# Idle transposes, early selectors and a value product beside the copies in the prologue of a four-layer kernel

## The chip, the cores and the metric

One core of a Trainium2 chip runs one program. The metric is the device time of one execution in microseconds, as the median of the runs. The engines are TensorE (PE; its weight loads are shown as PEld), VectorE (DVE), ScalarE (ACT), GpSimd (POOL) and the sync engine (SP), which issues most transfers.

## The reference, cut to what matters

Four sequences of 512 tokens of width 256 go through four layers: a causal attention block (L0), a small expert adapter (L1), a routed feed-forward block (L2), and an attention block with bias, mask and a scale and shift made from a time step (L3). The change lies in the start of L0 for sequence 0 and in the sine embedding of L3.

```python
def _L0_cond_ref(x, gate_score, Wq, bq, Wk, bk, Wv, bv, ...):
    h = layernorm(x, gamma1, beta1)
    Q, K, V = h @ Wq + bq, h @ Wk + bk, h @ Wv + bv      # 16 heads of 16
    scores = Q K^T / 4, causal
    ctx = softmax(scores) @ V
    ...
def _L3_cond_ref(src, src_mask, timestep, attention_bias, W_ada, ...):
    emb = silu(_sin_emb(timestep)) @ W_ada + b_ada       # scale and shift of L3
    x = _ln(src) * (1.0 + scale) + shift
    ...
```

## The kernel before, in words

The work is laid out by ticks. A tick from 0 on is a unit: one head of one block of 128 query tokens; an attention has 64 units, and there are eight attentions (four sequences, two layers with attention). In each unit every engine takes its standing work (scores and transposes on TensorE, the maximum on VectorE in `maxima`, the exponential on ScalarE, copies of the transposed probabilities on one of the last two), and then the dense steps that the plan put on that tick with `at(tick, engine, step, ...)`. Every engine runs its own list strictly in order; semaphores join them. Ticks below 0 are the prologue, which has dense steps alone. `copy_sides` decides from the planned loads which engine copies in which unit.

The prologue of before, for sequence 0:
- `plan_norm(-20, ...)` on VectorE: statistics (L998), a chain of small instructions for the inverse root, and `apply` (L1039), which writes h in four pieces.
- `turn_tokens` (L1236): eight transposes of h into dense banks 0 and 1, then `feature_half` on VectorE and ScalarE, which writes hT.
- `qk` 0 and 1 (L1258): the Q and K products of the first eight heads, 4 matmuls each, then `v` 0 (L1272), the value product of the first two blocks of tokens, 8 matmuls. The other Q and K products, `qk` 2 and 3, come at ticks 2 and 3.
- The Q and K rows are split into three bf16 parts: `hi` (ScalarE, L860), `rest` (VectorE, L1076), `mid` (ScalarE, L865), `lo` (VectorE, L1082).
- `restack` (L1367): 48 small matmuls with selection matrices put the parts of the first 256 tokens into eight banks. ScalarE copies four banks to `qs` (L893) and signals early_q_done, VectorE copies four to `ks` (L968) and signals early_k_done. `selectors` (L958 to L962) makes the selection matrices from the identity: a memset, a reduction, 16 small copies.
- `v` 1 (L1272): the value product of the other two blocks. It needs dense bank 0, which holds one of the four K banks of the restack, and waits for all four K copies. `values_out` (L1092) copies it out.
- `setup_sin` on ScalarE (L899, L901) takes a sine and an exponential of a small table that GpSimd has made; each needs a table load. Its result is read by `setup_silu` at tick 20.
- GpSimd makes the identity first (L649, L650), then clears `va` (L657, L658), and then works on the angles (L671 to L698).

scores(0) waits for all eight copies of the restack. The norm of sequence 1 starts at tick -1 and its `qkv0` at tick 6. Banks: `score_bank` is bank 0 and 1, `turn_bank` 2 and 3, `ctx_bank` 4, `dense_bank` 5 to 7.

Of the kernel before, what the change touches and what calls it, by code (L numbers as in the profile page):

```python
# [27 lines left out]
P = 128  # L28
# [63 lines left out]
def at(tick, engine, step, *args):  # L92
    EVENTS.append((tick, engine, step, args))


def plan_norm(t, s, k):


    for i in range(2):
        at(t + i, "v", "stats", s, k, i)  # L100
    for i in range(RSQRT_STEPS):
        at(t + 2 + i // SLOTS, f"v{i % SLOTS}", "rsqrt", s, k, i)
    for i in range(2):
        if k in (3, 4, 5):
            at(t + 3 + i, "v", "apply", s, k, i)
            at(t + 5 + i, "v", "apply_late", s, k, i)
        else:
            at(t + 5, "v", "apply", s, k, i)
    if k == 1:
        at(t + 6, "p", "res_l0", s)  # L110
    if k == 6:
        at(t + 6, "p", "res_l3", s)


def plan_turn(t, s, k):
    at(t, "pe", "turn_tokens", s, k)
    at(t + 1, "v", "feature_half", s, k)
    at(t + 1, "a", "feature_half", s, k)


def plan_qkv(t, s, l, second=6, late=4):

    for c in range(2):
        for i in (2 * c, 2 * c + 1):
            u = t + second * c
            at(u + i % 2, "pe", "qk", s, l, i)
            at(u + 1, "a", "hi", s, l, i)
            at(u + 2, "v", "rest", s, l, i)
            at(u + 3, "a", "mid", s, l, i)
            at(u + 4, "v", "lo", s, l, i)  # L130
            at(u + 4, "sp", "parts", s, l, i)
    at(t + 2, "pe", "v", s, l, 0)
    at(t + 3, "v", "v", s, l, 0)
    at(t + late, "pe", "v", s, l, 1)
    at(t + late + 1, "v", "v", s, l, 1)


def plan_ffn(t, s, f):
# [14 lines left out]
        at(t + i + 1, "v", "residual", s, l, i)  # L153


def qkv0(t, s, second=6, late=4):

    plan_turn(t, s, 0)
    plan_qkv(t + 3, s, 0, second, late)


def block0(t, s):
# [23 lines left out]
def qkv3(t, s):  # L186

    plan_turn(t, s, 4)
    plan_qkv(t + 3, s, 1)
# [9 lines left out]
def norm(k):  # L199
    return lambda t, s: plan_norm(t, s, k)  # L200
# [3 lines left out]

STACKS_AT = [(-2, 11)] + [(-28, 4)] * 2 + [(-20, 4)] + [(-28, 4)] * 3 + [(-20, 4)]
BESIDE = [
    [(-1, norm(0), 1), (6, qkv0, 1), (24, norm(0), 2)],
    [(11, qkv0, 2), (12, norm(1), 0), (23, block0, 0), (48, norm(3), 0), (55, block2, 0)],
    [(8, norm(4), 0), (15, norm(5), 0), (22, norm(1), 1), (23, qkv3, 0), (35, block0, 1), (42, norm(0), 3), (60, norm(3), 1)],
    [(3, block2, 1), (20, norm(4), 1), (23, qkv0, 3), (27, norm(1), 2), (34, norm(5), 1), (36, block0, 2), (61, norm(3), 2)],  # L210
    [(11, qkv3, 1), (12, norm(6), 0), (23, block2, 2), (40, block3, 0), (41, norm(4), 2), (48, norm(5), 2)],
    [(11, qkv3, 2), (12, norm(1), 3), (23, block0, 3), (48, norm(3), 3), (55, block2, 3)],
# [7 lines left out]
        at(UNITS * _a + _t, "sp", "stack", _s, _l, _c)  # L220
plan_norm(-20, 0, 0)
at(-14, "v", "setup_scale")
qkv0(-14, 0, 13, 8)
at(-12, "v", "selectors")
at(-12, "a", "setup_sin")
for _e in ("pe", "v", "a"):
    at(-6, _e, "restack")
at(20, "v", "setup_silu")
# [111 lines left out]
def build(nc, T, out):  # L340
    with ExitStack() as ctx:
        def sb(name, shape, dt=F32):
            return ctx.enter_context(nc.sbuf_tensor(name, shape, dt))

        def sem(name):
            return ctx.enter_context(nc.semaphore(name))


        ident = sb("ident", [P, P])
# [79 lines left out]
        score_bank, turn_bank, ctx_bank, dense_bank = bank[0:2], bank[2:4], bank[4], bank[5:8]  # L429
# [11 lines left out]
        early_k_done = sem("early_k_done")  # L441
# [56 lines left out]
        def unit(U):  # L498

            a, u = divmod(U, UNITS)  # L500
            l = ATTENTIONS[a][1]
            c, t, e, j = u // (2 * NT * GH), u // (2 * GH) % NT, u // GH % 2, u % GH
            return a, l, c, t, e, j, HH * c + 2 * j + e, (t + 1) * P if l == 0 else S
# [5 lines left out]
        def prob_of(U):  # L509

            _, l, _, _, _, _, _, n = unit(U)
            return prob[:, U % 3, 0:n] if l == 0 else bias[:, bias_pair(U) % BIAS_RING, U % 2, :]

        early_q_bank = [score_bank[0], score_bank[1], turn_bank[0], turn_bank[1]]
        early_k_bank = [ctx_bank, dense_bank[2], dense_bank[0], dense_bank[1]]

        def res_count(s, layer):

            name, n = {0: ("res_l0", 2), 2: ("res_l2", 1), 3: ("res_l3", 1)}[layer]
            total = 0  # L520
            for _, _, step, args in sorted((t, i, st, a) for i, (t, e, st, a) in enumerate(EVENTS)
                                           if e == "p" and st.startswith("res")):
                total += NT * (2 if step == "res_l0" else 1)
                if step == name and args[0] == s:
                    return total
# [685 lines left out]
        def _(pe):  # L1211
# [51 lines left out]
            def v_rows(s, l, i):  # L1263
                if ATT[s, l] == 0:
                    pe.wait_ge(load_v, 16 * LOADS_V)
                    if i:
                        pe.wait_ge(early_k_done, 4)
                if i:
                    pe.wait_ge(rest_done, 4 * ATT[s, l] + 2)
                for t in (2 * i, 2 * i + 1):  # L1270
                    for c in range(ND):
                        mm = pe.matmul(dense_bank[V_BANK[i]][:, (t % 2) * D:(t % 2 + 1) * D], hT[:, c, t * P:(t + 1) * P],  # L1272
                                       wv[l][:, c, :], start=c == 0, stop=c == ND - 1)
                mm.then_inc(v_psum, 1)
# [82 lines left out]
            def restack():  # L1357
# [4 lines left out]
                for side, banks, signal in ((0, early_q_bank, early_q), (1, early_k_bank, early_k)):  # L1362
                    for e in range(2):
                        for x in range(3):
                            for g in range(4):
# [3 lines left out]
                                if x == 2 and e == 1:  # L1369
                                    mm.then_inc(signal, 1)  # L1370

            def scores(U):
                a, l, c, t, e, j, hd, n = unit(U)
                if U == 0:
                    pe.wait_ge(early_q_done, 4)
                    pe.wait_ge(early_k_done, 4)
                if U == 2 * HH or U % (UNITS // 2) == 0 and U:
                    pe.wait_ge(stack_in[hd // HH], 96 * (a + 1))
                if U >= 2:
                    pe.wait_ge(p_done if unit(U - 2)[1] == 0 else max_done, U - 1)  # L1380
                mm = pe.matmul(score_bank[U % 2][:, 0:n], qs[:, hd, t * P:(t + 1) * P], ks[:, hd, 0:n],  # L1381
                               start=True, stop=l == 1)
                if l == 0:
                    mm = pe.matmul(score_bank[U % 2][:, n - P:n], identb[:], causal[:], start=False, stop=True)  # L1384
                mm.then_inc(s_psum, 1)
# [32 lines left out]
            def spread_sums(p):  # L1418
# [4 lines left out]
                for w in range(2):  # L1423
# [2 lines left out]

            steps = dense_steps("pe")
            do = {"turn_tokens": turn_tokens, "qk": qk, "v": v_rows, "project": project, "hidden": hidden,
                  "ff_out": ff_out, "turn_expert": turn_expert, "down": down, "expert": expert, "up": up, "setup": setup, "restack": restack}
            pe.wait_ge(consts, 2)  # L1430
            for U in range(FIRST, max(LAST + 1, ALL_UNITS + NORM_AT + 1)):
                if U == 0:
# [59 lines left out]
```

## Time and profile before

| | |
|---|---|
| median of 3 runs | 1169.03 us (1167.12 to 1172.2) |
| the profiled execution | 1163.56 us, span of its instructions 1161.5 us |
| mean granted TensorE clock | 0.959 of full speed |
| PE busy | 997.7 us, 86% of the span |
| VectorE busy | 730.8 us, 63% |
| ScalarE busy | 694.2 us, 60% |
| GpSimd busy | 454.1 us, 39% |

Times of the trace count from the first instruction. A busy PE is not a PE at its peak. The granted clock is in parts of full speed, 0.5 is 1.2 GHz and 1.0 is 2.4 GHz; until about 15 us the record shows 1.00, while the matmuls' durations are those of the low level.

### The profile page before, as it was taken

What the parts mean: (1) busy time and instruction counts of PE and PEld (TensorE: products, weight loads), DVE (VectorE), ACT (ScalarE), POOL (GpSimd) and SP (SyncE); (2) the same over time, 40 slices, a digit from 0 to 9 for tenths busy, and PEclk for the clock granted to TensorE, in tenths of its full rate; (3) what the DMA queues carried; (4) which work ended last, traced back from release to release, by engine and by line L of the source; (5) the groups of instructions that cost most, each with busy time, mean ns of one, the idle gap of its engine ahead of it and who ended that gap; (6) DMA issues with size and microseconds to landing.
All of it is one profiled execution on the core that took longest, in us unless ns stands there. A gap on an engine that the chain in (4) does not pass through costs nothing.

```text
span 1161.5 us, 22288 instructions
## 1 busy us (share of the span) xinstructions
PE 997.7 (86%) x7668; PEld 658.7 (57%) x7668; DVE 730.8 (63%) x1964; ACT 694.2 (60%) x1608; POOL 454.1 (39%) x694
## 2 busy tenths in 40 slices
PE   4878889897889898798889998897996899799768
PEld 3435557465556575466546565575573557557545
DVE  5677773737755738846773668638649864764750
ACT  3566564664675755676565755656754775675731
POOL 8300020000530374561072006847737564894920
PEclk8899999998999998899999999899897899999989
DMA  6868425133261634854626128575393387944600
GB/s 175 224 157 187 74 73 113 34 84 62 63 140 46 146 122 127 198 177 149 130 75 148 37 90 209 183 166 194 104 226 104 121 225 224 219 141 150 214 1 19
DMA packets 118354, 154.79 MB, mean 133 GB/s; under 512 B 12956, under 2 KB 80924, under 8 KB 118244
## 3 DMA queue, kind: packets, MB, share of 16 engines
q1 hardware_dynamic: 113636, 147.04, 47.3%
q0 software_dynamic: 1936, 3.97, 1.4%
q10 hardware_dynamic: 2672, 2.36, 0.6%
q8 instruction: 63, 1.03, 0.4%
q14 instruction: 47, 0.39, 0.1%
HBM read 134.47 MB, written 18.88 MB: 132 GB/s over the span
## 4 chain that ended last, share of the span: by engine, by line
PE 51%; DVE 18%; ACT 15%; issue 9%; DMA 4%; POOL 4%; DVEq 0%; ACTq 0%; POOLq 0%
PE bank L1307 14%; PE bank L1296 9%; PE bank L1399 7%; PE bank L1258 5%; PE bank L1413 5%; PE bank L1381 4%; POOL bias L798 4%; DMA bias<-in_fside_Bx16xSxS 3%; DVE mrow L1142 3%; ACT gT L874 3%; DVE bias L1148 3%; ACT bias L827 2%; ACT prob L824 2%; ACT L874 2%; ACT L827 2%
## 5 line engine op out<-in xcount | busy, mean ns | idle before, releaser
L798 POOL TENSOR_TENSOR bias<-bias,negmask 128x256 f32<-128x256 f32 x512 | 335.9, 687 | 259.2 <-DMA bias<-in_fside_Bx16xSxS 252.6
L827 ACT ACTIVATE bias<-bias,mrow 128x512 f32<-128x512 f32 x256 | 184.1, 719 | 209.3 <-DVE mrow L1148 207.8
L1148 DVE CUSTOM_DVE_ANT_0 bias<-bank,bias 128x512 f32<-128x512 f32 x256 | 175.4, 687 | 186.5 <-PE bank L1381 175.3
L824 ACT ACTIVATE prob<-bank,mrow 128x128 f32<-128x128 f32 (+3 forms) x256 | 134.7, 527 | 193.1 <-DVE mrow L1142 191.6
L1142 DVE TENSOR_REDUCE mrow<-bank 128x1 f32<-128x128 f32 (+3 forms) x256 | 124.5, 488 | 164.5 <-PE bank L1384 163.1
L1381 PE MATMUL bank<-ks,qs 128*128 128x512 bf16 (+3 forms) x512 | 180.3, 352 | 49.2 <-ACT prob L824 34.5
L1399 PE MATMUL bank<-ident,bias 128*128 128x128 f32 x1024 | 164.7, 286 | 54.0 <-ACT pT L835 43.8
L1399 PEld LDWEIGHTS bank<-ident,bias 128*128 128x128 f32 x1024 | 125.2, 146 | 123.9 <-ACT bias L827 71.3
L1296 PE MATMUL bank<-hT,w 128*128 128x512 f32 x384 | 182.6, 606 | 2.0 <-ACT hT L851 0.9
L1307 PE MATMUL bank<-w,gT 128*128 128x256 f32 x768 | 174.3, 381 | 0.0
L1307 PEld LDWEIGHTS bank<-w,gT 128*128 128x128 f32 x768 | 142.5, 190 | 20.2 <-issue 2.7
L1156 DVE COPY pT<-bank 128x512 f32<-128x512 f32 (+3 forms) x237 | 136.5, 576 | 6.4 <-PE bank L1399 5.9
L835 ACT ACTIVATE pT<-bank 128x512 f32<-128x512 f32 (+3 forms) x275 | 139.9, 509 | 1.1 <-PE bank L1399 1.1
L1399 PE MATMUL bank<-ident,prob 128*128 128x128 f32 x640 | 117.9, 283 | 14.2 <-ACT pT L835 8.8
L1413 PE MATMUL bank<-pT,va 128*32 128x128 f32 x3328 | 124.1, 287 | 4.4 <-DVE ctxn L1175 3.3
L1381 PEld LDWEIGHTS bank<-ks,qs 128*128 128x128 bf16 x512 | 50.5, 99 | 127.0 <-ACT prob L824 62.9
L1413 PEld LDWEIGHTS bank<-pT,va 128*32 128x32 f32 x3328 | 87.7, 114 | 28.1 <-issue 25.6
L1296 PEld LDWEIGHTS bank<-hT,w 128*128 128x128 f32 x384 | 68.3, 194 | 61.4 <-issue 59.7
L1399 PEld LDWEIGHTS bank<-ident,prob 128*128 128x128 f32 x640 | 70.9, 144 | 38.5 <-issue 28.9
L757 POOL TENSOR_TENSOR x<-x,xy 128x256 f32<-128x256 f32 x16 | 13.0, 842 | 154.1 <-DVE h L1039 154.1
L768 POOL TENSOR_TENSOR xy<-xy,l2row 128x256 f32<-128x256 f32 x16 | 12.1, 786 | 145.5 <-PE bank L1236 145.5
L874 ACT ACTIVATE gT<-bank,b 128x512 f32<-128x512 f32 x96 | 59.9, 685 | 10.2 <-PE bank L1296 9.8
(155 smaller groups left out, 1140.6 us busy)
## 6 DMA issues: line engine op xcount, KB each, us to landing
bias<-in_fside_Bx16xSxS SPq DMA_DIRECT2D x128, 512.0 KB, 4.6
w<-in_L_cond_W SPq DMA_DIRECT2D x16, 1024.0 KB, 5.6
qs<-q_parts SPq DMA_DIRECT2D x30, 384.0 KB, 10.3
ks<-k_parts SPq DMA_DIRECT2D x30, 384.0 KB, 11.7
q_parts<-parts SPq DMA_DIRECT2D x80, 128.0 KB
k_parts<-parts SPq DMA_DIRECT2D x48, 128.0 KB
w<-in_L_cond_Wi SPq DMA_DIRECT2D x4, 1024.0 KB, 5.0
w<-in_L_cond_Wo SPq DMA_DIRECT2D x4, 1024.0 KB, 5.6
```

The lines of the kernel that those rows point to most:

```text
L798: pool.tensor_tensor(b_n, b_n, negmask[:, t, keys], ALU.add).then_inc(masked, 1)
L824: act.activation(prob_of(U), score_bank[U % 2][:, 0:n], ACT.Exp, bias=mrow[:, U % ROW_RING:U % ROW_RING + 1], accum_out=rsum[:, U % ROW_RI ...
L827: act.activation(prob_of(U), prob_of(U), ACT.Exp, scale=-1.0, bias=mrow[:, U % ROW_RING:U % ROW_RING + 1], accum_out=rsum[:, U % ROW_RING: ...
L835: act.activation(pT[:, U % PT_RING, 0:n // P, :], turn_bank[U % 2][:, 0:n].rearrange("p (k q) -> p k q", q=P), ACT.Identity).then_inc(pt_a, 1)
L1142: v.tensor_reduce(m, score_bank[U % 2][:, 0:n], AX_X, ALU.max, negate=True).then_inc(max_done, 1)
L1148: v.tensor_tensor_reduce(out=prob_of(U), in0=score_bank[U % 2][:], in1=prob_of(U), scale=-1.0, scalar=3e38, op0=ALU.add, op1=ALU.min, accu ...
L1156: v.tensor_copy(pT[:, U % PT_RING, 0:n // P, :], turn_bank[U % 2][:, 0:n].rearrange("p (k q) -> p k q", q=P)).then_inc(pt_v, 1)
L1296: mm = pe.matmul(dense_bank[FF_BANK[j]][:], w1[:, c, j * P:(j + 1) * P], hT[:, c, :], start=c == 0, stop=c == ND - 1)
L1307: mm = pe.matmul(dense_bank[FF_OUT_BANK[t // 2]][:, (t % 2) * D:(t % 2 + 1) * D], gT[:, j, t * P:(t + 1) * P], w2[:, j, :], start=j == 0, ...
L1381: mm = pe.matmul(score_bank[U % 2][:, 0:n], qs[:, hd, t * P:(t + 1) * P], ks[:, hd, 0:n], start=True, stop=l == 1)
L1399: mm = pe.transpose(turn_bank[U % 2][:, k * P:(k + 1) * P], prob_of(U)[:, k * P:(k + 1) * P], ident[:])
L1413: mm = pe.matmul(ctx_bank[32 * j:32 * (j + 1), t % 2 * P:(t % 2 + 1) * P], v_h, pT[:, (GH * w + j) % PT_RING, k, :], start=e == 0 and k == ...
```

## The change

`selectors` moves from tick -12 to tick -21, ahead of the norm of sequence 0. `setup_sin` moves from tick -12 to -5, behind the restack's copies on ScalarE. TensorE gets a new step, `idle_turns`, which transposes the identity into the first score bank; nothing reads the result. It stands at tick -15 with 28 transposes and at tick -8 with 10. The banks of the early K copies change places, so that dense bank 0 is copied first, and `v` 1 waits for one K copy and not for four. The copy-out of `v` 1 for sequence 0 moves from tick -2 to tick 2 (the new argument `copy`). The norm of sequence 1 moves from tick -1 to 2, and its `qkv0` from 6 to 8. With the plan's loads the side of the copies changes in 11 of the first 20 units.

```diff
-def plan_qkv(t, s, l, second=6, late=4):
+def plan_qkv(t, s, l, second=6, late=4, copy=1):
...
     at(t + late, "pe", "v", s, l, 1)
-    at(t + late + 1, "v", "v", s, l, 1)
+    at(t + late + copy, "v", "v", s, l, 1)
...
-def qkv0(t, s, second=6, late=4):
+def qkv0(t, s, *places):
...
-    plan_qkv(t + 3, s, 0, second, late)
+    plan_qkv(t + 3, s, 0, *places)
...
-    [(-1, norm(0), 1), (6, qkv0, 1), (24, norm(0), 2)],
+    [(2, norm(0), 1), (8, qkv0, 1), (24, norm(0), 2)],
...
-qkv0(-14, 0, 13, 8)
-at(-12, "v", "selectors")
-at(-12, "a", "setup_sin")
+qkv0(-14, 0, 13, 8, 5)
+at(-15, "pe", "idle_turns", 28)
+at(-8, "pe", "idle_turns", 10)
+at(-21, "v", "selectors")
+at(-5, "a", "setup_sin")
...
-        early_k_bank = [ctx_bank, dense_bank[2], dense_bank[0], dense_bank[1]]
+        early_k_bank = [dense_bank[0], ctx_bank, dense_bank[2], dense_bank[1]]
...
                     if i:
-                        pe.wait_ge(early_k_done, 4)
+                        pe.wait_ge(early_k_done, 1)
...
+            def idle_turns(n):
+
+                for _ in range(n):
+                    pe.transpose(early_q_bank[0][:, 0:P], ident[:], ident[:])
```

## Rows read from the trace of the kernel before

**Rows 1.** The page: the chain that ended last, by engine.

```profile
PE 51%; DVE 18%; ACT 15%; issue 9%; DMA 4%; POOL 4%; DVEq 0%; ACTq 0%; POOLq 0%
```

**Rows 2.** The chain in order of time, first 80 us: start us, length us, what.

```profile
4.41 1.42 DVE stats L998 x4
...
9.21 1.96 PE bank L1236 x8
...
12.18 5.18 PE bank L1258 x8
17.35 1.74 PE bank L1272 x8
19.21 0.76 DVE va L1092 x2
19.97 1.21 DVE parts L1082 x2
21.23 2.02 PE bank L1367 x48
...
25.95 3.42 PE bank L1272 x8
29.49 0.76 DVE va L1092 x2
30.24 0.66 DVE stats L998 x2
...
31.13 0.47 ACT prob L824 x2
```

**Rows 3.** Timeline, VectorE and ScalarE: start us, us, engine line op out<-in xcount.

```profile
12.18 0.70 DVE L958 MEMSET bias<- 128x768 uint32 x1
13.33 1.58 DVE L962 CAST bias<-bias 128x32 bf16<-128x32 f32 x16
14.86 1.28 ACT L901 ACT_TABLE_LOAD   x1
16.16 0.21 ACT L901 ACTIVATE bias<-bias 128x8 f32<-128x8 f32 x1
22.19 2.06 ACT L893 ACTIVATE qs<-bank 128x512 bf16<-128x512 f32 x4 [2.67 <-PE bank L1367]
23.36 2.48 DVE L968 CAST ks<-bank 128x512 bf16<-128x512 f32 x4 [2.19 <-PE bank L1367]
```

**Rows 4.** Timeline, GpSimd and VectorE at the start.

```profile
1.54 1.38 POOL L657 MEMSET va<- 128x1536 f32 x1
9.88 0.64 POOL L682 TENSOR_SCALAR bias<-bias 128x4 f32<-128x4 f32 x1
9.94 0.43 DVE L951 TENSOR_SCALAR wq<-wq 128x512 f32<-128x512 f32 x1
```

**Rows 5.** Line L1236 to 14 us (duration ns min/median/max, first and last start); four K products.

```profile
L1236 PE MATMUL bank<-ident,h x8: 421/421/447, 9.2 to 10.7; 128*128 128x128 f32 x8
...
47.58 1.88 PE L1258 MATMUL bank<-hT,wk 128*128 128x512 f32 x4
```

**Rows 6.** Windows: length, PE, PEld, DVE, ACT, POOL busy (x), PEclk, DMA share, GB/s.

```profile
18.60:22.00 3.40, 1.25 (x31) 0.82 (x33) 2.22 (x5) 0.63 (x1) 3.40 (x6) 1.00 0.67 193
22.00:25.40 3.40, 1.25 (x28) 0.60 (x16) 2.04 (x4) 2.06 (x4) 3.40 (x7) 0.51 0.72 159
990.00:1004.00 14.00, 11.37 (x134) 7.89 (x135) 11.71 (x31) 10.86 (x27) 13.03 (x20) 1.00 0.80 210
```

**Rows 7.** The last of these windows, transposes of the probabilities (L1399) alone.

```profile
990.00:1004.00 14.00, 7.32 (x48) 4.99 (x46) 1.00 0.80 210
```

**Rows 8.** Timeline: qk 2 at unit 2, and the first maximum over 256 keys (unit 8).

```profile
31.88 3.22 PE L1258 MATMUL bank<-hT,wq 128*128 128x512 f32 x4
...
43.81 0.41 DVE L1142 TENSOR_REDUCE mrow<-bank 128x1 f32<-128x256 f32 x1
```

**Rows 9.** Window of units 0 to 7, from the first exponential to unit 8's maximum.

```profile
31.10:43.80 12.70, 9.83 (x45) 4.80 (x45) 9.13 (x35) 6.55 (x25) 6.71 (x10) 0.82 1.01 220
```

More of the change, by code:

```diff
@@ L1428, in _ @@
             do = {"turn_tokens": turn_tokens, "qk": qk, "v": v_rows, "project": project, "hidden": hidden,
-                  "ff_out": ff_out, "turn_expert": turn_expert, "down": down, "expert": expert, "up": up, "setup": setup, "restack": restack}
+                  "ff_out": ff_out, "turn_expert": turn_expert, "down": down, "expert": expert, "up": up, "setup": setup, "restack": restack, "idle_turns": idle_turns}
             pe.wait_ge(consts, 2)
```

## The prediction

> **What bounds the kernel now.** I read the page's chain first: half of it is TensorE, a fifth VectorE, 9% issue [rows 1]. After the first tokens no single engine sets the pace; that stretch is bounded by hand-overs, and the diff leaves it alone but for the planner's first 30 ticks. So a gain can only be a start of attention 0 that comes earlier and is then carried through. Next I read the chain of the first 80 us in order of time [rows 2]. The reader should see four pieces ahead of the first exponential at 31.13: the norm of sequence 0 (4.41 to 9.21), twelve us of products and their splitting into parts (to 21.23), the restack products with the four K copies behind them (to 25.95), then a value product of 3.42 us with its copy (0.76) and half of the next sequence's statistics (0.66) on VectorE, before which the first maximum can't run. The last two pieces are 9.9 us long and most of what they hold is an order, not a dependency. All of it is judged against the profiled execution, 1163.56 us (span 1161.5); the median of the three runs is 1169.03, 5.5 higher, and I take the saving off that.
>
> **Selectors first.** The same 18 instructions move from 12.18 to the front of VectorE's queue, where they wait for the identity alone. They take 2.73 us: from the memset at 12.18 to the end of the sixteenth copy, 13.33 + 1.58 = 14.91 [rows 3]. The identity is there at 1.5 (GpSimd's next instruction starts at 1.54 [rows 4]), so they end at about 4.3, and the statistics start at 4.41 on a transfer: cost 0. They were not on the chain where they stood (14.91 is long before 21.23), so removing them gains 0 too. The cover is thin, 0.1 us. Beside them GpSimd now runs two memsets of 1.38 us, from 1.54 on [rows 4]. The trace doesn't show that pairing. It does show that the two engines can hold each other up: a GpSimd instruction on 128x4 took 0.64 us at 9.88, as VectorE scaled 128x512 in SBUF at 9.94 [rows 4]. Bounds: 0, and one memset's length, 1.4 us, ahead of the statistics. I take 0, because in their old place the copies kept an even pace of 0.1 us each beside GpSimd's small instructions [rows 3]; 1.4 is a rival. On this the Trainium skill (SBUF — State Buffer, section Summary: rules for kernel authors) says that a VectorE instruction in a two-port mode and a GpSimd one block each other completely, the later one waiting for the end of the first; by it the copies would wait for the second memset and the sum would be 1.4 us worse. The trace agrees on the small GpSimd instruction, and shows nothing of the reverse.
>
> **28 turns of the identity.** Eight transposes of this size began between 9.2 and 10.7, 0.214 us apart, at the low clock [rows 5]. So 28 take 6.0 us, from 1.5 to 7.5, before the tokens come at 9.21: they delay nothing unless each takes over 0.27 us (a lone one is recorded with 0.42 [rows 5]). Do they make the first products fast? Four Q products with four K products took 5.18 us in the chain while four at the full clock take 1.88 [rows 2, 5], so the first four ran at 1.2 GHz; at 2.4 they would give 1.7 us, and the token turns 0.7 (1.96 us for what then follows the tokens within 0.3 us each). Upper bound 2.4 us. But between 7.5 and 9.2 TensorE idles, or longer if the clock rises on the way and the turns end sooner, then works in small pieces on the tokens and idles again until hT is there, 12.18 [rows 2]. What idling does is in the trace: after v(0) ended at 19.1 the engine stood until 21.23, and the granted clock, 1.00 until 22.0, was 0.51 after it [rows 6]. I take 0 of the 2.4 us: the clock rises under the turns and is gone before the products. Then the start at 12.18, the high clock from about 15, v(0), the splitting, and the restack at 21.23 all stay.
>
> **setup_sin behind the copies.** ScalarE's two table loads (1.28 us each) and two small activations (0.21 each) [rows 3] leave 12 to 16.4. The first hi may start sooner for it, but the chain goes from both products (to 17.35) through v(0) to VectorE [rows 2], past ScalarE's wait, so 0. In their new place they follow the Q copies, which end at 22.19 + 2.06 = 24.25 [rows 3]: 2.98 us, to 27.25. Its output is wanted at tick 20 only. Queued behind it is the first exponential.
>
> **10 turns.** They fill 19.1 to 20.2 of the gap before the restack (10 x 0.107 at the high clock), delaying nothing. The idle time there falls from 2.1 to 1.0 us, and I expect the clock to stay high: the restack products (2.02, the second half at the low clock [rows 2, 6]) give back 0.4 us (0 to 0.6), and v(1) takes 1.74 as v(0) did, not 3.42 [rows 2].
> Whether turns hold the clock at all is a question of its own. From 990 to 1004 it stood at 1.00 while 7.3 of 11.4 busy us were transposes [rows 6, 7]: they at least don't break it. The Trainium skill (TensorE: Matmul & The Clock Gate, section Part 4: PE-mode transpose) says that the full clock doesn't engage for transposes, which don't count as a busy engine the same way. By that rule neither set of turns does anything; this is a rival below. The trace doesn't decide it, since matmuls stand between those transposes.
>
> **v(1) beside the K copies.** It now waits for one K copy, not four, since the bank that it needs is copied first. The four take 2.48 us [rows 3]. With the restack 0.4 earlier they run from 22.95 to 25.45; v(1) starts at 23.65 and ends at 25.4, hidden. scores(0) comes at 25.5, where v(1) alone ended at 25.95 + 3.42 = 29.37 before: 3.8 less.
>
> **The VectorE queue ahead of the first maximum.** The values' copy (tick -2 to 2) and the norm of sequence 1 (tick -1 to 2) go behind it. So the maximum runs at 25.8 to 26.1, where it ended at about 31.1: 5.0 earlier. Here setup_sin becomes the later one: the exponential starts at 27.25 and not at 31.13. Saved at this point: 3.9 us, and 1.15 us of the maximum's lead is lost to the table loads.
>
> **What it costs later.** 0.76 us of copy and the norm of a sequence (for sequence 0 it took 4.8 us from first statistics to tokens [rows 2]) now lie in units 2 to 7, three ticks later, qkv0(1) two ticks later. Before, most of the norm lay under four products of 3.22 us at the low clock [rows 8], which held the scores back; after them it lies where VectorE has the splitting to do as well. Bounds: -1.0 (the clock stays high under those products and more than pays for it) and 2.5 (half the norm comes into the open). I take 0.6: from 31.1 to 43.8, units 0 to 7, VectorE was busy for 9.1 of 12.7 us [rows 9], so most of it finds room. SP's queue: the parts of (1,0) are issued two ticks later, wanted in attention 1 only.
> Sum: 3.9 - 0.6 = 3.3 saved. 1163.56 - 3.3 = 1160.3 beside the profiled run, 1169.0 - 3.3 = **1165.7** as a median.
>
> **The rivals.**
> *The clock lasts into the first products*: 2.4 us more, all else the same; saved 5.7, 1163.3. For it: only small gaps stand between 9.2 and 12.2. Against it: the fall at 22.0.
> *GpSimd's memset holds the selectors*: 3.3 - 1.4 = 1.9 saved, 1167.1. Against it: no VectorE instruction of this trace's beginning is stretched.
> *Turns don't count*: the restack stays as it is, v(1) runs from 24.1 for 3.42 to 27.5, the first exponential at 28.1: 3.0 - 0.6 = 2.4 saved, 1166.6. The small difference is because setup_sin would have eaten that time anyway.
> *The displaced norm is exposed* (the slower side): values' copy and norm, 0.76 + 4.8 = 5.6 us, lie on VectorE between unit 2 and the tokens of sequence 1, whose products every later unit waits behind. If all of it is in the open, 3.9 - 5.6 = 1.7 lost, 1170.7. It decides from the point at which over 3.9 of the 5.6 us are uncovered. Against it: in the 12.7 us before unit 8's maximum (43.81 [rows 8]) VectorE had 3.6 us free [rows 9], with most of the norm already in its work.
>
> **How the numbers follow.** Forecast 0.43 (its own range 1163 to 1168.5), clock lasts 0.22, turns don't count 0.11, memset 0.12, norm exposed 0.12. 0.5% is 5.8 us, about what a measurement of this kernel can tell from no change. Faster by more needs under 1163.2: half of the second case, the edge of the first and the -1.0 bound together, 0.21. Slower by more needs over 1174.9: only an exposed norm with a fallen clock, 0.04. Within: 0.75. The three runs shown differ by 5 us, so the range reaches past the cases: 1161 to 1170.5.
>
> **What would show it.** Right: statistics still at 4.4, the first Q product of 12.2 at half speed, restack at 21.2, scores(0) near 25.5, the first exponential directly behind the second table load near 27.3, unit 8's maximum 3 to 4 us before 43.8. Wrong: statistics at 5.8 (memset), a Q product that starts at 11.5 and takes 0.43 (clock lasts), v(1) of over 3 us (turns don't count), unit 8 no earlier than 43 (norm exposed). A saving of over 6 us at unit 8 would mean that I put too low what the clock gives back.

## The result, and the profile after

| | before | changed |
|---|---|---|
| median of 5 runs | 1167.19 us (1167.0 to 1172.2) | 1160.35 us (1157.17 to 1162.13) |
| ratio | | 0.9925 [0.99, 0.9951] |
| the profiled execution | 1163.56, span 1161.5 | 1160.35, span 1158.5 |

The changed kernel is 6.8 us faster where 3.3 were forecast: 0.6 us under the range's low end of 1161, and on the side to which I gave 0.21. The forecast median was 1165.7, 5.3 us above the measured one. Of these, 1.8 are the starting point (1169.03 from three runs, 1167.19 from five) and 3.5 are the saving itself. Beside the profiled run of before the difference is only 3.2 us, which looks like the forecast. It isn't, as the experiments show.

The page of the changed kernel, its span and its busy times:

```profile
span 1158.5 us, 22278 instructions
...
PE 988.7 (85%) x7619; PEld 664.2 (57%) x7706; DVE 730.7 (63%) x1961; ACT 695.4 (60%) x1611; POOL 452.6 (39%) x694
...
PE 44%; DVE 21%; ACT 15%; issue 9%; POOL 5%; DMA 4%; another core or an unknown queue 1%; SPq 0%; DVEq 0%; ACTq 0%; POOLq 0%
```

The 9 us less that TensorE is busy (988.7 against 997.7) are no saving: this trace has 7619 matmuls for 7706 weight loads, so 87 matmul records are missing, and none are in the trace of before (7668 of each). A second trace of before lacks 87 too and has 986.7. TensorE's share of the chain falls from 51% [rows 1] to 44%, but second traces of both kernels have 46%. The page tells little; the chain and the single units tell more.

The chain of the changed kernel in order of time, first 63 us (start, length, what); lines have moved by 2 against before:

```profile
2.85 2.45 DVE bias L964 x16
5.30 1.32 DVE stats L1000 x4
...
9.92 1.98 PE bank L1238 x8
...
12.91 6.59 PE bank L1260 x8
19.50 1.74 PE bank L1274 x8
...
23.38 0.94 PE bank L1369 x24
24.34 2.06 ACT qs L895 x4
26.42 1.28 ACT L901
27.94 1.28 ACT L903
29.45 0.36 ACT prob L826 x2
30.25 1.72 PE bank L1260 x4
...
62.80 1.88 PE bank L1349 x4
```

Three things differ from [rows 2]. The selectors' sixteen copies now stand in the chain ahead of the statistics, which start at 5.30, not at 4.41. The restack begins 2.15 us later than before (23.38 against 21.23). From there to the first exponential it takes 6.0 us (23.38 to 29.35) where before took 9.9, and v(1) and its copy are gone from it; the two table loads (L901, L903) are the last thing before the exponential.

Timeline of the same stretch, VectorE, GpSimd and TensorE (start, length, engine, line, operation, out<-in):

```profile
2.85 2.45 DVE L964 CAST bias<-bias 128x32 bf16<-128x32 f32 x16
2.94 1.53 DVE L964 CAST bias<-bias 128x32 bf16<-128x32 f32 x5
...
2.97 1.38 POOL L660 MEMSET va<- 128x1536 f32 x1
...
1.53 5.01 PE L1377 MATMUL bank<-ident 128*128 128x128 f32 x28 [1.53 <-POOL ident L652]
...
12.91 3.75 PE L1260 MATMUL bank<-hT,wq 128*128 128x512 f32 x4 [1.03 <-ACT hT L853]
...
23.38 1.49 PE L1369 MATMUL bank<-parts,bias 32*128 32x256 bf16 x48 [1.06 <-DVE parts L1084]
25.79 1.97 PE L1274 MATMUL bank<-wv,hT 128*128 128x256 f32 x8 [0.92 <-issue]
```

The second line is the same view in the window 3.3 to 4.36 us, and holds the five of the sixteen copies that are under way there. The reader should see the copies lasting 2.45 us beside a GpSimd memset, where they took 1.58 without one [rows 3], with five of them begun by 3.28 and done only at 4.38 to 4.47, right behind the memset's end at 4.35; 28 transposes in 5.0 us and the first Q product after them still at half speed (3.75 for four matmuls that take 1.88 at the full clock [rows 5]); and v(1) at 1.97, beside the K copies.

Where the time went shows best in the start of the exponential of a unit, in us. "Second trace" is the trace of the whole kernel run once more (`f_before2` and `f_after2` below, on two different chips); the last column is the normalisation (the write of ctxn) of the last attention:

| trace | unit 0 | unit 10 | unit 18 | unit 22 | unit 39 | last ctxn |
|---|---|---|---|---|---|---|
| before | 31.13 | 48.02 | 63.50 | 72.54 | 95.42 | 1114.55 |
| before, second trace | 30.76 | 47.65 | 63.14 | 72.19 | 95.09 | 1117.72 |
| changed | 29.35 | 43.65 | 57.66 | 66.13 | 87.95 | 1111.87 |
| changed, second trace | 27.87 | 42.34 | 58.23 | 66.71 | 88.65 | 1110.70 |

The changed kernel leads by 1.8 us at unit 0 (forecast: 3.9), 4.4 at unit 10, 5.8 at unit 18 and 7.5 at unit 39. So most of the gain arises after the prologue, in units 0 to 22, in the term for which I had put down a loss of 0.6. By stretches, this pair gains 2.3 us from unit 0 to 5, 0.3 to unit 10, 1.5 to unit 18, 0.6 to unit 22 and 1.1 to unit 39. From there the lead stays between 5.7 and 7.5 until 904 us, and then falls to 2.7 at 1114.55. That last fall is the luck of one execution of before: its second trace agrees with the first within 0.8 us up to 740 us, and is 3.2 us later at the last normalisation. Against it the leads of the changed kernel's two traces there are 5.9 and 7.0:

```profile
1114.55 0.42 DVE L1175 TENSOR_TENSOR ctxn<-bank,spread 128x256 f32<-128x256 f32 x1 [3.06 <-ACT spread L843]
```

```profile
1117.72 0.42 DVE L1175 TENSOR_TENSOR ctxn<-bank,spread 128x256 f32<-128x256 f32 x1 [3.11 <-ACT spread L843]
```

These are the last normalisations in the timelines of before and of its second trace.

### The profile page after: what moved, and what is told of

The parts are those of the page before. It is cut to its first block, busy times and chain, and to the rows that moved or that the text cites. A ratio compares the mean times of both kernels' runs of the same rounds, so it can differ in the third digit from the quotient of the medians.

```text
span 1158.5 us, 22278 instructions
## 1 busy us (share of the span) xinstructions
PE 988.7 (85%) x7619; PEld 664.2 (57%) x7706; DVE 730.7 (63%) x1961; ACT 695.4 (60%) x1611; POOL 452.6 (39%) x694
## 3 DMA queue, kind: packets, MB, share of 16 engines
q8 instruction: 63, 1.03, 0.4%
## 4 chain that ended last, share of the span: by engine, by line
PE 44%; DVE 21%; ACT 15%; issue 9%; POOL 5%; DMA 4%; another core or an unknown queue 1%; SPq 0%; DVEq 0%; ACTq 0%; POOLq 0%
PE bank L1309 14%; PE bank L1298 8%; PE bank L1406 6%; POOL bias L800 4%; PE bank L1260 4%; DMA bias<-in_fside_Bx16xSxS 4%; PE bank L1420 3%; DVE bias L1150 3%; DVE mrow L1144 3%; ACT gT L876 3%; PE bank L1388 3%; ACT bias L829 2%; DVE stats L1000 2%; ACT prob L826 2%; ACT L876 2%
## 5 line engine op out<-in xcount | busy, mean ns | idle before, releaser
L1388 PE MATMUL bank<-ks,qs 128*128 128x512 bf16 (+3 forms) x425 | 146.4, 345 | 45.6 <-ACT prob L826 32.5
```

## The experiments

The question became: which part makes the 7 to 8 us, and why in units 0 to 22? Most kernels here are cut to the prologue and the first 40 units, where a microsecond is 1% of the time and not 0.1%.

### First cut: the end was set by loads

In all four, every engine's loop ends at unit 40 and SP's at tick 36; at the end the tokens are stored as they were loaded. `s_noturns` has no `idle_turns`, `s_noplan` has the planner's line of before.

```diff
-at(-15, "pe", "idle_turns", 28)
-at(-8, "pe", "idle_turns", 10)
```

```diff
-    [(2, norm(0), 1), (8, qkv0, 1), (24, norm(0), 2)],
+    [(-1, norm(0), 1), (6, qkv0, 1), (24, norm(0), 2)],
```

> The kernel before, cut short: every engine leaves its list at unit 40 of the first attention (SP at tick 36), and the tokens as loaded are stored, so only the prologue and the first 40 units are computed. It is the ruler for the parts of the change. If what is gained lies in the prologue and the first 24 units, the time is 6.5 to 8 us above that of the changed kernel cut in the same way (the two profiles stood 7.5 us apart at unit 39); if the full kernel's gain is spread over later stages, the two lie under 5 us apart.

> The changed kernel, cut at unit 40 as the other. Gain in the first 40 units: 6.5 to 8 us below the cut kernel before. Gain elsewhere, or a matter of the clock's luck in one profile: 2 to 5 us below.

> The changed kernel cut at unit 40, with both sets of idle transposes taken out. Theory: the 10 before the restack keep the clock up, so that restack and v(1) run at 2.4 GHz; without them 1.5 to 2.5 us more than the cut changed kernel, and v(1) of over 3 us in the profile. Rival (transposes don't count, or v(1) hides either way): within 0.7 us of it. Rival (the 28 only shift the time at which the clock rises, and hurt): 1 us or more below it.

> The changed kernel cut at unit 40, with the norm of sequence 1 back at tick -1 and its qkv0 at tick 6. Theory of the prediction (the displaced norm costs 0.6 us): 0.6 us below the cut changed kernel. Rival (the later place is what gains 3 us between units 4 and 22, since it keeps the norm from standing before the first maxima and the products from holding up the scores): 1.5 to 3.5 us above it.

Medians: `s_before` 109.0, `s_after` 107.3, `s_noturns` 106.8, `s_noplan` 107.4 us. As times these say nothing. The timeline of ScalarE in `s_after` shows why: its last exponential starts at 86.56 and the store is issued only at 97.03, on loads that the cut kernel doesn't need.

```profile
86.56 0.37 ACT L826 ACTIVATE prob<-bank,mrow 128x128 f32<-128x128 f32 x1
...
97.03 3.40 ACTq L943 DMA_DIRECT2D out<-xy  x4
```

The traces of units are usable all the same. The last exponential starts at 94.85 in `s_before`, 86.56 in `s_after`, 88.23 in `s_noturns` and 91.40 in `s_noplan`: 8.3 us for all, of which the turns are 1.7 and the planner's line, on which I had put −0.6, is 4.8.

### Second cut: each part undone

SP now stops at tick 22 and the loads of biases and rows are not waited for. All of the following compute the prologue and 40 units only and store the tokens. The edits, each against the changed kernel (`t_after`):

```diff
# t_noplan: the planner's line as before
-    [(2, norm(0), 1), (8, qkv0, 1), (24, norm(0), 2)],
+    [(-1, norm(0), 1), (6, qkv0, 1), (24, norm(0), 2)],
# t_normback: the norm alone
-    [(2, norm(0), 1), (8, qkv0, 1), (24, norm(0), 2)],
+    [(-1, norm(0), 1), (8, qkv0, 1), (24, norm(0), 2)],
# t_vback: copy of v(1), K banks and wait as before
-qkv0(-14, 0, 13, 8, 5)
+qkv0(-14, 0, 13, 8)
-        early_k_bank = [dense_bank[0], ctx_bank, dense_bank[2], dense_bank[1]]
+        early_k_bank = [ctx_bank, dense_bank[2], dense_bank[0], dense_bank[1]]
-                        pe.wait_ge(early_k_done, 1)
+                        pe.wait_ge(early_k_done, 4)
# t_selback
-at(-21, "v", "selectors")
+at(-12, "v", "selectors")
# t_sinback
-at(-5, "a", "setup_sin")
+at(-12, "a", "setup_sin")
```

`t_noturns` leaves both `idle_turns` out. `t_planonly` is the other way round: before, with nothing but the planner's line of the changed kernel.

> The kernel before, cut at unit 40, and SP's list cut at tick 22, so that the loads of rows and of the bias are left out too (in the first cut they ended after the engines and set the time). Theory (the gain is made in the prologue and the first 24 units): its time is 7 to 9 us above that of the changed kernel cut in this way. Rival (the two profiles of the first cut differed by the clock's luck): 3 to 5 us.

> The changed kernel in the second cut. Theory: 7 to 9 us below the kernel before in this cut. Rival: 3 to 5 us below.

> The changed kernel in the second cut with norm and qkv0 of sequence 1 back at ticks -1 and 6. Theory (the later products of sequence 1 fill TensorE's idle time under the splitting at units 17 to 21): 3 to 4 us above the cut changed kernel, with unit 17 to 22 lasting 14 to 15 us and not 11 to 12, and TensorE idle for half of that. Rival (the first pair of profiles differed by a fall of the clock only): within 1.5 us.

> The changed kernel in the second cut with the norm of sequence 1 alone back at tick -1; its qkv0 stays at tick 8. If the place of the products is what gains: within 0.8 us of the cut changed kernel. If the norm in front of the first maxima is what costs: 1.5 to 3 us above it.

> The changed kernel, cut at unit 40 (second cut), without the 28 and the 10 idle transposes. The cut changed kernel took 97.26 us. Theory (the turns before the restack hold the clock up for the restack and v(1)): 1 to 2 us more, with a v(1) of over 3 us. Rival (transposes don't count as work): within 0.5 us. Rival (the 28 let the clock rise and fall before the tokens, and the first products start colder): 0.5 to 1.5 us less.

> The changed kernel in the second cut, with the second value product waiting for all four K copies again, the banks in the old order and its copy-out at tick -2. By the prediction's working scores(0) comes 1.8 us later (the product at full clock no longer under the copies) and VectorE's copy of 0.76 stands before the first maximum; of these 2.6 us about 1.2 are covered by setup_sin, so 1 to 1.8 us more than 97.26. Rival (setup_sin covers all of it): within 0.5 us.

> The changed kernel in the second cut with the selectors back behind hT at tick -12. The changed profile shows the 16 selector copies beside GpSimd's memset taking 2.45 us and not 1.58, and the statistics starting at 5.30 and not 4.41. Theory (moving them costs 0.9 us, since nothing waited for them where they stood): 0.5 to 1.2 us less than 97.26, statistics at 4.4. Rival (they held up the splitting where they stood, so that their move gains): 0.5 us or more above 97.26.

> The changed kernel in the second cut with setup_sin back at tick -12, ahead of the first hi. Theory (its two table loads now stand before the first exponential and cost 1 to 1.5 us there, while at the old place the chain ran past ScalarE): 0.8 to 1.6 us less than 97.26, with the first exponential right behind its maximum. Rival (at the old place it delays the first hi and with it the restack): 0.5 us or more above.

> The kernel before in the second cut (105.75 us) with one part of the change alone: norm and qkv0 of sequence 1 at ticks 2 and 8. Theory (the later products fill TensorE's idle time at units 17 to 21, whatever the prologue does): 3 to 4.5 us less than 105.75. Rival (the shift pays only where the first maximum comes early): under 1.5 us less.

Times in us. The differences are to `t_after`, for `t_planonly` to `t_before`, by the medians, by the lowest runs, and by the medians of the close runs, those within 1.5% of their kernel's lowest. Where the three disagree, the close runs decide. The runs of one such kernel spread over 1 to 5 us, so a difference under 1 us isn't settled; single runs far out (119.38 of `t_normback` here, below 220.13 of `t_more2` and 1942.26 of `f_before2`) count in the medians only. The first four were measured on one chip and the others on another. exp(0) and exp(39) are the starts of these exponentials in each kernel's one trace. The traces of `t_noplan`, `t_vback` and `t_selback` are of runs above their median (104.07, 102.2 and 97.6 us), so their exp(39) overstates the time; those of `t_normback`, `t_sinback` and `t_planonly` are of runs below it (96.35, 96.2 and 98.95), so theirs understates it.

| kernel | median | lowest | difference: median | lowest | close runs | exp(0) | exp(39) |
|---|---|---|---|---|---|---|---|
| t_before | 105.75 | 105.14 | +8.5 | +8.6 | +8.5 | 30.99 | 95.77 |
| t_after | 97.26 | 96.59 | | | | 28.36 | 86.71 |
| t_noplan | 101.62 | 100.58 | +4.4 | +4.0 | +4.2 | 29.48 | 93.76 |
| t_normback | 98.30 | 96.35 | +1.0 | −0.2 | −0.6 | 27.33 | 86.11 |
| t_noturns | 98.68 | 98.27 | +1.4 | +1.7 | +1.5 | 29.25 | 88.04 |
| t_vback | 101.13 | 98.67 | +3.9 | +2.1 | +1.6 | 30.77 | 91.97 |
| t_selback | 96.84 | 95.69 | −0.4 | −0.9 | −1.4 | 26.49 | 87.36 |
| t_sinback | 97.59 | 96.08 | +0.3 | −0.5 | −1.0 | 26.84 | 85.93 |
| t_planonly | 100.56 | 98.36 | −5.2 | −6.8 | −7.1 | 30.39 | 88.65 |

**The planner's line.** It is worth 4.2 to 4.4 us with the other parts and 5.2 to 7.1 alone, the largest part of the change, and nearly all of it comes from `qkv0` two ticks later: with the norm alone put back (`t_normback`) it costs 1.0 by the median, nothing by the lowest and the close runs. All twenty traces, cut and whole, agree: from exp(0) to exp(39) the six kernels with `qkv0` at tick 6 take 62.7 to 64.8 us, the fourteen with it at tick 8 take 58.2 to 61.2. The mechanism stands in the windows between the exponentials of units 5, 10, 18 and 22 (length; busy time of PE, PEld, DVE, ACT, POOL with counts; granted clock; DMA share; GB/s), first of `t_before`:

```profile
40.27:48.80 8.53, 6.61 (x29) 2.74 (x29) 3.99 (x11) 4.39 (x17) 2.16 (x2) 0.80 1.12 275
48.80:64.28 15.48, 13.82 (x90) 8.65 (x88) 10.54 (x25) 9.22 (x26) 0.00 (x0) 1.00 0.75 187
64.28:74.26 9.98, 8.39 (x48) 3.97 (x46) 4.91 (x12) 4.36 (x12) 0.00 (x0) 0.66 0.80 170
```

and the same of `t_planonly`:

```profile
37.51:44.66 7.15, 4.69 (x31) 3.20 (x31) 6.10 (x21) 4.83 (x18) 1.86 (x2) 0.76 1.14 203
44.66:58.67 14.01, 13.75 (x85) 8.63 (x86) 9.00 (x23) 7.87 (x25) 0.00 (x0) 1.00 0.65 216
58.67:67.16 8.49, 7.50 (x55) 3.96 (x53) 6.13 (x14) 5.65 (x15) 0.00 (x0) 1.00 1.10 183
```

In the second stretch TensorE has the same 13.8 us of work in both, but idles for 1.66 us in `t_before` and for 0.26 in `t_planonly`. In the third it has 7 matmuls less in `t_before`, yet is busy for longer, because the granted clock is 0.66 and not 1.00. The chain of `t_before` tells what lies there:

```profile
58.92 1.91 PE bank L1270 x4
...
62.80 1.09 issue
63.89 0.51 PE bank L1411 x3
...
64.86 1.13 ACT parts L865 x2
...
70.00 2.80 PE bank L1359 x4
```

and that of `t_planonly`:

```profile
58.38 1.72 PE bank L1270 x4
...
63.82 1.88 PE bank L1359 x4
```

In `t_before` the last K product of sequence 1 (58.92) is done before unit 18. Then ScalarE and VectorE split it into parts, the units wait behind them (the row "issue" at 62.80, the split at 64.86), TensorE has no dense work and idles in gaps of 0.6 to 1.1 us, its clock falls, and the setup's products (L1359) take 2.80 for what takes 1.88 at the full clock. With `qkv0` two ticks later the same product runs at unit 18, its splitting lies beside the setup, and the clock stays at 1.00. Both deep stretches shrink, by 1.5 us each; in the first, 8.53 to 7.15, the first Q product of sequence 1 runs at the low clock in `t_before` (3.52 at 44.55) and at the high one in `t_planonly` (1.78 at 45.33). `t_noplan` has the lengths of `t_before` again (8.78, 15.91, 10.26) and `t_after` those of `t_planonly` (7.22, 14.01, 8.48).

How much of this the whole kernels have: 7.35, 15.48 and 9.04 before, 7.10, 14.01 and 8.47 after, so 0.3, 1.5 and 0.6 us. The trace of before shows the same order of things as `t_before`, with a shorter fall of the clock; its chain, and its window from exponential 18 to 22:

```profile
62.02 1.08 issue
...
64.08 1.13 ACT parts L865 x2
...
68.70 2.38 PE bank L1347 x4
```

```profile
63.50:72.54 9.04, 7.32 (x48) 3.60 (x46) 4.91 (x12) 4.36 (x12) 0.00 (x0) 0.81 0.86 163
```

The 14.01 is no certainty either. The middle stretch took 13.6 to 14.0 us in twelve of the fourteen traces with `qkv0` at tick 8, but 15.9 in `f_after2` and `t_selback`, where the first Q product took 3.62 us; `f_after2`'s granted clock is 0.50 from 36.3 to 46.5 us.

The windows begin at unit 5 and leave out units 0 to 5, where the whole pair gains 2.3 us (9.54 to 7.20) and `t_planonly` gains 2.2 on `t_before` (9.28 to 7.12). About 0.7 of it is the place of the norm: `t_normback` and `t_noplan` take 7.84 there and `t_after` 7.15. Most of the rest is the Q product of unit 2, which ran at the low clock in three of the four traces of before, whole and cut (3.14 to 3.22 us), and took 1.88 in the fourth (`s_before`, 7.87). Whether the planner's line keeps the clock up there, or these three traces met a fall that it has nothing to do with, no run shows.

**v(1) beside the copies.** Put back, it costs 3.9 us by the median, 2.1 by the lowest and 1.6 by the close runs, of which only the last lies in the expected 1 to 1.8. TensorE then waits 2.7 us for the K copies, and v(1) doesn't keep the clock even with the 10 turns in front of the restack. Timeline of TensorE in `t_vback`:

```profile
22.72 1.49 PE L1381 MATMUL bank<-parts,bias 32*128 32x256 bf16 x48 [1.06 <-DVE parts L1096]
26.92 2.73 PE L1286 MATMUL bank<-wv,hT 128*128 128x256 f32 x8 [2.72 <-issue]
```

**The turns.** Without any of them 1.4 to 1.7 us are lost, but the trace of `t_noturns` doesn't show why. Its v(1) took 1.97 all the same (over 3 was expected), after an idle time of 2.15 us where `t_after` has 1.06, and 0.8 of the 0.9 us by which its first exponential is later is the length of the first eight products (6.38 against 5.57), which varies as much in traces with the turns. In `s_noturns`, the same edit, v(1) took 3.75. So what shows of the 10 turns is steadiness: v(1) took 1.97 in all twelve traces that have them and v(1) beside the copies, and in one of the two that have v(1) there without them. The whole kernel before has it both ways without them, 3.40 in its first trace and 1.97 in its second. The 28 do nothing for the products: the first Q product took 3.35 to 3.75 us in twelve traces with them, and 3.46 to 3.75 in seven without. They sometimes help the eight token transposes before it, which took 1.40 to 1.42 us in four of the twelve, 1.66 in one, and 1.92 to 1.97 in the others and in all seven without.

**The selectors.** In their old place the sixteen copies take 1.55 us again and the statistics start at 4.27. Timeline of VectorE in `t_selback`:

```profile
4.27 1.41 DVE L1012 BATCH_NORM_STATS2 stats<-xy 128x6 f32<-128x256 f32 x4 [4.27 <-DMA xy<-in_x]
...
12.57 1.55 DVE L976 CAST bias<-bias 128x32 bf16<-128x32 f32 x16
```

The statistics are 1.03 us earlier than in `t_after` (5.30), and the time is 0.4 to 1.4 us less: this part of the change is a small loss.

**setup_sin.** Put back, the exponential of unit 0 follows the maximum directly (26.84 behind 26.51). From the first K copy (23.57) to it are 3.3 us, in the changed kernel 4.35 (25.00 to 29.35): 1.1 us are exposed in the new place. The time hardly settles whether they last (+0.3 by the median, −0.5 by the lowest, −1.0 by the close runs; 0.8 to 1.6 less was expected).

### Doing more, and doing less

`t_best1` takes both small losses back; `t_more2` adds turns enough to bridge the gaps that the 28 leave. `f_best1` is `t_best1` as a whole kernel, `f_after2` and `f_before2` are the changed kernel and the one before, whole, once more.

```diff
# t_best1, f_best1, t_more2
-at(-21, "v", "selectors")
-at(-5, "a", "setup_sin")
+at(-12, "v", "selectors")
+at(-12, "a", "setup_sin")
# t_more2 beside it
-at(-15, "pe", "idle_turns", 28)
+at(-15, "pe", "idle_turns", 48)
+at(-12, "pe", "idle_turns", 8)
```

> The changed kernel in the second cut (97.26 us) with selectors and setup_sin both back at tick -12. Theory (the first costs 0.9 us beside GpSimd's memset, the second 1.2 us ahead of the first exponential): the first exponential 2 us earlier, near 26, and 1.5 to 2 us less than 97.26. Rival (what is won there is lost in units 0 to 20, which wait for other things): within 0.7 us.

> As the last, with 48 idle transposes in place of 28 and 8 more between the token turns and the first product, so that TensorE hardly idles from 1.5 us to the first product. Theory of the prediction (the 28 bring nothing because the clock falls again in the gap before the tokens): with the gap filled the first Q product runs at 2.4 GHz, 1.9 us long and not 3.5, and the time is 1.5 to 2.5 us under the kernel without them. Rival (transposes can't hold the clock): 3.5 us long, the same time or 0.5 us more.

> The changed kernel whole, once more, for a second trace of it. The first stood 6.4 us ahead of the kernel before from unit 22 to about 870 us and only 2.7 at 1100. If the late loss is the clock's luck in that execution: another pattern of falls after 870 us, and a distance at 1100 us of over 4 us. If it belongs to the change: again under 3.5.

> The kernel before, whole, for a second trace of it. Its profiled execution was 1163.56 us, 3.6 under the median of its runs, and the changed kernel's two traces both lose 2.5 to 3.7 us of their lead to it late. If that trace was a lucky one in its late part: the second trace reaches unit 22 as late as the first (within 1 us), but its last quarter is 1.5 to 4 us longer. If the late loss belongs to the change: the second trace ends like the first, within 1 us at 1100.

> The changed kernel, whole, with selectors and setup_sin back at tick -12, all else as changed. The cut kernels stood 2.1 us apart (95.12 and 97.26). If a lead at unit 39 is carried to the end: 1 to 3 us less than the changed kernel's 1159.5 to 1160.35, 1157 to 1159. If it is lost in units that wait for transfers: 1159 to 1161.

`t_best1`: 95.12 us median, 94.02 lowest, 2.1 (2.6) under `t_after`; exp(39) at 83.69. `t_more2`: 95.19 and 93.48, the same median and 0.5 under it by the lowest run, where 1.5 to 2.5 were expected. Its timeline on TensorE:

```profile
1.53 7.27 PE L1390 MATMUL bank<-ident 128*128 128x128 f32 x48 [1.53 <-POOL ident L653]
9.06 1.41 PE L1251 MATMUL bank<-ident,h 128*128 128x128 f32 x8 [0.26 <-DVE h L1054]
10.31 1.04 PE L1390 MATMUL bank<-ident 128*128 128x128 f32 x8
11.50 1.95 PE L1273 MATMUL bank<-hT,wq 128*128 128x512 f32 x4 [0.16 <-ACT hT L854]
...
19.89 1.49 PE L1382 MATMUL bank<-parts,bias 32*128 32x256 bf16 x48 [1.91 <-DVE parts L1097]
```

The first Q product takes 1.95 and not 3.4 to 3.75. This is the clock that the 28 turns were after, and it is worth at most 0.5 us here. The products and v(0) are done by 16.9, but the chain of `t_more2` then goes through GpSimd's angles and the second table load to the splitting, and the restack starts at 19.89, only 0.7 earlier than in `t_best1`:

```profile
14.22 0.21 ACT bias L902
...
14.45 1.28 ACT L904
15.74 0.21 ACT bias L904
15.95 0.59 ACT parts L863
```

ScalarE can't begin the splitting before its second table load is over, although the first Q product is done at 13.45. With `setup_sin` in its new place, behind the copies, the fast product might be worth more; I didn't run that.

The whole kernels: `f_after2` 1159.5 us, ratio 0.9911 [0.9885, 0.9937]; `f_before2` 1169.43, ratio 1.0009 [0.9987, 1.0032]; `f_best1` 1157.61, ratio 0.9895 [0.9864, 0.9926]. The gain of the change thus repeats. `f_best1` is the fastest of them, by 1.9 us on its median, but its interval overlaps with that of the changed kernel, and it was measured on another chip than `f_after2`; its exponential of unit 39 starts at 86.08, where the two traces of the changed kernel have 87.95 and 88.65.

## Why the prediction was wrong, and where it was right

**What it costs later: the failed step.** I took a loss of 0.6 us within −1.0 to 2.5. Measured in the cut kernels: a gain of 4.4 us beside the other parts, 5.2 alone. In the whole pair the lead grows by 4.6 us from unit 0 to 22. The sign was wrong, and even my best bound reached a quarter of it. The step asked where VectorE would find room for the displaced norm, and looked at units 2 to 7 only [rows 9]. The norm's place is nearly without effect (`t_normback`), as that reasoning would have it. What I passed over is the other half of the same line, `qkv0` from 6 to 8. I costed it as a delay and didn't ask where its last products end. Rows of the trace of before, shown above, would have told: the chain from 60 to 70 us shows the splitting on ScalarE between two idle stretches of TensorE, and the granted clock is 0.50 from 66.4 to 69.8. The case of my −1.0, that the clock stays high under the products of unit 2, did come, and was too small as well: units 0 to 5 gained 2.3 us in the whole pair, though how much of that is the change's is open. The sign I had named, "a saving of over 6 us at unit 8 would mean that I put too low what the clock gives back", looked in the right direction and at the wrong place: at unit 8 the maximum came 3.2 us earlier (40.62 against 43.81), at unit 22 the lead was 6.4.

**Selectors first: 0, measured about 0.7 to 1.0 on the chain.** The statistics moved from 4.41 to 5.30, and `t_selback` gets 1.03 back there. The rival had the mechanism, at 1.4 us: behind the first copy, those begun between 2.94 and 3.28 us end only at 4.38 to 4.47, behind the end of GpSimd's second memset (2.97 to 4.35), and the ten that follow take 0.17 each again. The same five stand still in all eleven traces with the selectors in front, and none in the nine without. The cost is 0.9 and not 1.4 because the five were already under way and came out together. The memset kept its 1.38 us. The Trainium skill (SBUF — State Buffer, section Summary: rules for kernel authors) says that of a VectorE instruction in a two-port mode and a GpSimd one the second waits until the first is done. No trace shows in which mode these copies run, but this one agrees with the rule: it is a standstill, not a slower pace. My reason for 0, that the copies had kept their pace beside GpSimd's small instructions, was an inference from 128x4 operations to one of 128x1536.

**28 turns: 0, right, for the reason given.** The first Q product says so (3.35 to 3.75 in all twelve traces with them), and so does the granted clock, 0.50 from 8.7 to 18.7 us in the changed kernel. `t_more2` supplies the other half: with the gaps bridged the granted clock doesn't fall before 32 us, and the product takes 1.95. What I left out is that the token transposes gained 0.5 us in four of the twelve. "The clock lasts" failed as a rival for this kernel.

**Turns don't count: refuted.** In `t_more2` 48 transposes took 7.27 us; at the low pace of 0.214 each [rows 5] they would take 10.3. After nothing but transposes the first product ran at full speed. The rule of the Trainium skill (TensorE: Matmul & The Clock Gate, section Part 4: PE-mode transpose), that the full clock doesn't engage for transposes, is contradicted by these rows for float transposes of 128x128.

**10 turns and v(1) beside the copies: right in length.** From the start of the restack to the first exponential the forecast had 6.02 us; it was 5.97. The restack took 1.49 and v(1) 1.97, hidden under the copies, as forecast. Undone singly the turns cost 1.4 us and v(1) 3.9 (1.6 by the close runs), together 3.0 to 5.3 around the 3.9 of the forecast. What the low clock took from before was partly that one trace: its second trace has the restack at 1.49 and v(1) at 1.97 without any turns.

**setup_sin: right in size.** Forecast 1.15 us exposed before the first exponential, measured 1.1.

**The lead at unit 0: 1.8, not 3.9.** Two things ate it in the profiled pair: the selectors (0.9, of which 0.7 is left at the first products, 12.91 against 12.18), and the first eight products, which took 6.59 us against 5.18 [rows 2]. The second isn't the change's: that length was 5.06 to 6.72 in traces with the 28 turns and 5.17 to 6.63 without. In the second pair of traces the lead is 2.9, with this luck the other way (5.11 against 6.63).

**The displaced norm exposed: refuted.** It had 0.12 and would have given 1170.7, slower than before.

**What stays open.** The single parts, undone one by one, add up to 9.6 us by the medians, 6.4 by the lowest and about 5 by the close runs, against 8.5 for all, so either they depend on each other or the spread of the runs hides their sizes; I tested one pair only: selectors and `setup_sin` singly give 1.4 and 1.0 by the close runs, and both together 2.2 (`t_best1`). The 2.3 us of units 0 to 5 have no run of their own. That the low clock is the cause of the third stretch rather than its companion is read from durations of the same products (2.80 against 1.88), not from a run in which the clock alone was changed. And that the late fall of the lead belongs to one trace of before rests on two traces of each kernel.

## What to carry to other kernels

Before costing a step that moves dense work between ticks, mark in the trace where TensorE idles and where its granted clock falls, over the whole stretch that the step reaches, and ask which of those gaps the work will fill: here two ticks were worth about half of the gain of the cut kernels (4.4 of 8.5 us). A single profiled execution can lie several microseconds beside the median, so compare the starts of the same unit in both traces, not the totals. With useless transposes in a short wait the product that followed within about a microsecond ran at the full clock in twelve traces of twelve, without them in one of two; where 3.4 us of idle time followed the 28, they bought the products nothing. Before moving VectorE work, look at what GpSimd does at that time: a large memset held small copies still until it was over.

## What the runs showed of the hardware that I had not expected

- Sixteen VectorE copies of 128x32 from float to bf16 took 2.44 to 2.46 us beside a GpSimd memset of 128x1536, 1.50 to 1.59 without one. The whole difference is a standstill: copies begun at 2.94 to 3.28 us ended at 4.38 to 4.47, behind the memset's end at 4.35. The memset took 1.38 both times, and VectorE's own memset of 128x768 took 0.70 beside GpSimd's first memset as without one.
- Transposes alone raise the granted pace: 28 from idle took 4.8 us in `t_best1` and 5.0 in the changed kernel, and 48 took 7.27, where the low pace alone would give 6.0 and 10.3. In one trace of twelve (`t_vback`) the 28 took 6.17, the low pace throughout.
- Idle stretches of 0.6, 1.1 and 0.6 us, one after another with about half a microsecond of work between, stood ahead of the granted clock's fall to 0.5 at 65.1 us in `t_before`. A single idle stretch of 2.15 us went both ways: the clock fell behind it in the first trace of before and not in `f_before2` or `t_noturns`.
